# Edge softmax of a GNN layer: one product before the score matmuls in place of two behind them

## The reference, cut to what matters

```python
w_m = (efeat @ W_msg + b_msg).reshape(E, in_f, -1)
w_a = (efeat @ W_attn + b_attn).reshape(E, in_f, -1)
h_src = feat[src][:, :, None]
e1 = w_m * h_src
e2 = w_a * h_src
seg_max = jax.ops.segment_max(e2, dst, num_segments=N)
ex = jnp.exp(e2 - seg_max[dst])
denom = jax.ops.segment_sum(ex, dst, num_segments=N)
attn = ex / denom[dst]
ft = jax.ops.segment_sum(e1 * attn, dst, num_segments=N)
return ft.sum(axis=1)
```

## Time and profile before

| | us |
|---|---|
| three runs: median, lowest, highest | 5352.39, 5348.31, 5366.21 |
| the profiled execution's own time | 5326.47 |
| its span | 5324.7 |
| busy in it: PE, DVE, POOL, ACT | 3185.9, 3431.4, 3310.8, 1667.5 |
| first and last maximum scan (L1617) start | 51.7 and 1320.6 |

### The profile page before, as it was taken

How to read it: one execution, slowest core, us unless ns; L and a number is a source line. 1 busy time by engine, 2 the same in 40 slices (tenths; PEclk the granted TensorE clock), 3 DMA queues, 4 the chain that set the end, 5 groups by cost and what they waited for, 6 DMA issues and landing times. The chain is left out here.

```text
span 5324.7 us, 56203 instructions
## 1 busy us (share of the span) xinstructions
PE 3185.9 (60%) x12749; PEld 2452.6 (46%) x12749; DVE 3431.4 (64%) x5617; ACT 1667.5 (31%) x4309; POOL 3310.8 (62%) x2831
## 2 busy tenths in 40 slices
PE   6999999998344444199923223622223635566676
PEld 3444444444244444188822223522223425556675
DVE  7999999999765555588833334633334854444478
ACT  4666666666221111055510000210000331111135
POOL 4777777776478888799965654066553245555322
PEclk9999999999865555599955556855565655555588
DMA  3111111111333333523200000310000220000012
GB/s 105 44 44 44 44 44 46 45 44 29 111 73 59 59 59 57 91 63 85 73 15 5 6 5 4 95 14 5 5 5 3 76 72 5 6 5 6 4 55 78
DMA packets 399126, 224.63 MB, mean 42 GB/s; under 512 B 106218, under 2 KB 369198, under 8 KB 398978
## 3 DMA queue, kind: packets, MB, share of 16 engines
q1 hardware_dynamic: 279698, 203.40, 13.3%
q0 software_dynamic: 119296, 19.68, 6.2%
HBM read 158.12 MB, written 64.76 MB: 42 GB/s over the span
## 5 line engine op out<-in xcount | busy, mean ns | idle before, releaser
L1333 PE MATMUL ps<-arena 128*128 128x128 f32 x2976 | 659.0, 408 | 1061.8 <-DVE arena L1854 658.4
L1333 PEld LDWEIGHTS ps<-arena 128*128 128x128 f32 x2976 | 608.5, 310 | 1099.3 <-issue 1088.3
L758 POOL DMA_INDIRECT extra<-x_t,srci x784 | 760.4, 970 | 538.2 <-DVE arena L1871 277.5
L1237 PE MATMUL ps<-edge_in,wl 17*128 17x512 f32 x784 | 701.9, 1072 | 17.4 <-DVE arena L1623 8.7
L742 POOL DMA_INDIRECT sums<-cmb,sidx x392 | 613.9, 1566 | 139.1 <-issue 115.1
L758 POOL DMA_INDIRECT extra<-h_t,srci x392 | 370.7, 946 | 413.8 <-issue 293.6
L704 POOL DMA_INDIRECT xg<-in_x,xidx x392 | 478.5, 1221 | 221.0 <-issue 116.0
L691 POOL DMA_INDIRECT ft_t<-fts,fidx x392 | 507.7, 1295 | 143.4 <-issue 120.3
L1871 DVE TENSOR_TENSOR arena<-arena,ps 128x128 f32 x1488 | 426.9, 287 | 247.0 <-issue 69.6
L1017 ACT ACTIVATE ps<-extra 128x16 f32 x1392 | 165.1, 170 | 1314.4 <-issue 687.0
L1854 DVE TENSOR_TENSOR arena<-jmask,ps 128x1024 f32<-128x1024 f32 (+1 forms) x174 | 212.4, 1221 | 513.2 <-issue 316.1
(11 more groups left out here) (244 smaller groups left out, 6227.9 us busy)
## 6 DMA issues: line engine op xcount, KB each, us to landing
edge_in<-far_row SPq DMA_DIRECT2D x98, 256.0 KB
ain<-in_src_row SPq DMA_DIRECT2D x56, 448.0 KB
sums<-zero SPq DMA_DIRECT2D x132, 144.0 KB
arena<-rel_t SPq DMA_DIRECT2D x63, 256.0 KB
x_t<-yout SPq DMA_DIRECT2D x28, 448.0 KB, 3.4
xin<-x_t SPq DMA_DIRECT2D x28, 448.0 KB, 4.0
extra<-x_t,srci POOLq DMA_INDIRECT x784
ain<-x_t SPq DMA_DIRECT2D x28, 448.0 KB, 5.2
```

Source lines behind the costliest of these rows:

```text
L758: pool.indirect_dma_start(dy[:, t, :], None, table, bass.IndirectOffsetOnAxis(ap=srci[:, t:t + 1], axis=0)).then_inc(d_gathered[n % QUEUE] ...
L1237: last = pe.matmul(ps[k][:, h * ET:(h + 1) * ET], wl[:, (k * CH + h) * P:(k * CH + h + 1) * P], eft[b][:, :], start=True, stop=True)
L1333: last = pe.matmul(slot_sums(k, n)[:, j * P:(j + 1) * P], oneh[b][:, j * P:(j + 1) * P], placed[b][:, j * P:(j + 1) * P], start=True, stop ...
```

## The change

`h_src[i] * efeat[f]` is now formed once, before the matmuls: DVE multiplies the replicated features (`ps2`) by the edge features, which are loaded eight times over, on 128 rows (`make_outer`). PE contracts these 128 rows against `wl` for both scores, and adds the bias by two bf16 matmuls with the turned features, on 128 rows too (the bias in parts, `bias_first` and `bias_last`). DVE has no product behind either score. ACT no longer copies `ps2` to `hS`; its inverse goes into `ps2` instead, which the replication of a later tile overwrites only after the ratio has read it. The turned features are made twice (at rows 0 and 64 of zeroed buffers). The steps move: replication and attention scores are one tile ahead, turning two. ACT copies the carry columns ahead of the turned rows. The gather moves to even steps. Weights and turned features live in buffers of later stages.

```diff
 # SP
-            sp.dma_start(wl[:, :], wlog).then_inc(cst_in, 16)
-            sp.dma_start(repf, repcon).then_inc(cst_in, 16)
+            for j in range(PACK):
+                sp.dma_start(wl[j * F:(j + 1) * F, :], wlog[0:F, :]).then_inc(cst_in, 16)
+            sp.dma_start(bias_raw, wlog[F:F + 1, :].broadcast_to((P, 2 * CH * P))).then_inc(cst_in, 16)
+            wait(repf_zero, 1)
+            for r in part_bases:
+                sp.dma_start(repf[r:r + PARTS * F, :], repcon).then_inc(cst_in, 16)
...
-                    sp.dma_start(eft[b][:, :], ef[:, bass.ds((2 * i + c) * ET, ET)]).then_inc(main_in[b], 16)
+                    sp.dma_start(eft[b], ef[0:F, bass.ds((2 * i + c) * ET, ET)]
+                                 .unsqueeze(0).broadcast_to((PACK, F, ET))).then_inc(main_in[b], 16)
 # POOL
-                if c % 2:
-                    gather(i, c + 3)
+                if c % 2 == 0:
+                    gather(i, c + 4)
 # ACT, in step: removed
-                    act.wait_ge(h_ps, n + 1)
-                    if later(i, c, 1):
-                        act.wait_ge(e1_done, n)
-                    act.activation(flat(hS), ps[2][:, :], ACT.Copy).then_inc(h_sb, 1)
 # ACT, in step: behind the four activations of tile n
+                if inside(i, c - 2, TILES):
+                    act.wait_ge(ln_done, 2 * i + c - 2 + 1)
+                    if later(i, c - 2, 1):
+                        act.wait_ge(rat_done, 2 * i + c - 2)
+                    act.wait_ge(outer_done, 2 * i + c + 2 if inside(i, c + 1, TILES) else TILES)
+                    act.activation(inv, lnd[:, :, :], ACT.Exp, scale=-1.0).then_inc(inv_done, 1)
+                if c % 2:
+                    cast_x(i, c + 3)
 # PE, in step
+                replicate(i, c + 1)
+                transpose(i, c + 2)
+                scores(i, c + 1)
                 if inside(i, c, TILES):
...
+                    products(1, b).then_inc(e1_ps, 1)
+
+            def products(k, b):
+
+                for h in range(CH):
+                    o = ps[k][:, h * ET:(h + 1) * ET]
+                    cols = slice((k * CH + h) * P, (k * CH + h + 1) * P)
+                    pe.matmul(o, wl[:, cols], outer[b][:, h * ET:(h + 1) * ET], start=True, stop=False)
+                    pe.matmul(o, bias_first[:, cols], xT[b][:, :], start=False, stop=False)
+                    last = pe.matmul(o, bias_last[:, cols], xT[b][:, :], start=False, stop=True)
+                return last
 # DVE, in step
-                if c % 2:
-                    split(i, c + 1)
+                if c % 2 == 0:
+                    split(i, c + 2)
...
-                    dve.tensor_tensor(ps[0][:, :], ps[0][:, :], flat(hS), ALU.mult).then_inc(e2_done, 1)
...
-                    dve.wait_ge(wm_ps, n + 1)
-                    dve.tensor_tensor(flat(e1[b]), ps[1][:, :], flat(hS), ALU.mult).then_inc(e1_done, 1)
+                make_outer(i, c + 1)
...
-                    dve.scalar_tensor_tensor(body(qq), body(uu[o]), 1.0, e1[o], ALU.mult, ALU.mult).then_inc(q_done, 1)
+                    dve.wait_ge(e1_ps, m + 1)
+                    dve.scalar_tensor_tensor(body(qq), body(uu[o]), 1.0, e1p, ALU.mult, ALU.mult).then_inc(q_done, 1)
+            def make_outer(i, c):
...
+                dve.wait_ge(h_ps, n + 1)
+                dve.wait_ge(main_in[b], 32 * (nth(i, c) + 1))
+                if later(i, c, 2):
+                    dve.wait_ge(e1_ps, n - 1)
+                dve.tensor_tensor(outer[b].rearrange("p (h e) -> p h e", h=CH),
+                                  ps[2][:, :].rearrange("p (h e) -> p h e", h=CH),
+                                  eft[b].unsqueeze(1).broadcast_to((P, CH, ET)), ALU.mult).then_inc(outer_done, 1)
```

More of the change, by code:

```diff
@@ L892, in copy_xT @@
                 act.wait_ge(xT_ps, 2 * i + c + 1)
-                if later(i, c, 1):
-                    act.wait_ge(h_ps, 2 * i + c)
-                act.activation(xT[:, :], ps[3][0:PARTS * F, 0:ET], ACT.Copy).then_inc(xT_sb, 1)
+                if later(i, c, 2):
+                    act.wait_ge(e1_ps, 2 * i + c - 1)
+                for r in part_bases:
+                    last = act.activation(xT[c % 2][r:r + PARTS * F, :], ps[3][r:r + PARTS * F, 0:ET], ACT.Copy)
+                last.then_inc(xT_sb, 1)
             act.preload_act_table_set("natural_log_exp_and_others")
@@ L1227, in step @@
[L1227 to L1240, removed]
@@ new lines, in replicate @@
+            def replicate(i, c):
+                if not inside(i, c, TILES):
+                    return
+                n = 2 * i + c
+                pe.wait_ge(xT_sb, n + 1)
+                if later(i, c, 1):
+                    pe.wait_ge(outer_done, n)
+                if later(i, c, 4):
+                    pe.wait_ge(rat_done, n - 3)
+                for h in range(CH):
+                    last = pe.matmul(ps[2][:, h * ET:(h + 1) * ET], repsel[:, h * P:(h + 1) * P], xT[c % 2][:, :],
+                                     start=True, stop=True)
+                last.then_inc(h_ps, 1)
@@ L1243, in transpose, with scores @@
+            def scores(i, c):
+                if not inside(i, c, TILES):
+                    return
+                n = 2 * i + c
+                pe.wait_ge(outer_done, n + 1)
+                if later(i, c, 1):
+                    pe.wait_ge(w_done, n)
+                else:
+                    pe.wait_ge(w_made, TYPES)
+                    pe.wait_ge(bias_w, 10)
+                products(0, c % 2).then_inc(e2_ps, 1)
             def transpose(i, c):
@@ L1251, in transpose @@
                 for k in range(SUB):
-                    last = pe.matmul(ps[3][0:PARTS * F, k * P:(k + 1) * P],
-                                     high(xq[:, c % 2 * SUB + k, :, :].rearrange("p a f -> p (a f)")), identb[:, :],
-                                     start=True, stop=True)
+                    parts = high(xq[:, c % 2 * SUB + k, :, :].rearrange("p a f -> p (a f)"))
+                    for r in part_bases:
+                        last = pe.matmul(ps[3][r:r + PARTS * F, k * P:(k + 1) * P], parts, identb[:, :],
+                                         start=True, stop=True)
                 last.then_inc(xT_ps, 1)
             transpose(0, 0)
+            transpose(0, 1)
             turn_slots()
+            replicate(0, 0)
+            scores(0, 0)
             softmax_steps(pe, step)
@@ L1475, in _ @@
             dve.memset(eps_col[:, :], EPS).then_inc(zero_made, 1)
+            dve.memset(repf, 0.0).then_inc(repf_zero, 1)
+            for b in range(2):
+                dve.memset(ain[b][:, 0:ET // 2], 0.0).then_inc(repf_zero, 1)
             dve.memset(zero[:, :], 0.0).then_inc(zero_made, 1)
```

92 lines of the change are left out of this document (59 added, 33 removed).

## The result

| | before | after |
|---|---|---|
| median (lowest to highest), us | 5351.7 (4 runs beside the changed kernel) | 5291.2 (5249.7 to 5298.4, 4 runs) |
| ratio, 95% interval | | 0.987 (0.985 to 0.990) |
| profiled execution, its span | 5326.5, 5324.7 | 5295.6, 5293.8 |
| busy PE, DVE, POOL | 3185.9, 3431.4, 3310.8 | 2930.6, 3324.2, 3301.5 |
| first maximum scan starts | 51.7 | 53.7 |

The changed kernel is 60 us faster; 49 were forecast. The stage ends 59.5 us earlier. In the profiled executions the whole program gained only 31: the first weight load of L1420 (L1375 before) still starts 58.6 us earlier, at 2204.5, the last of L1378 (L1333 before) only 27.4, at 5070.6. The change touches nothing between them, the medians show the 60, and the four times of the changed kernel lie 49 apart, so that is taken as variation between executions; no run shows it apart.

What follows compares the result with a forecast made beforehand. The prediction took DVE to bound the softmax stage, at 26.25 us per two tiles. 5326.5 - 133 (product gone) + 72 (POOL binds) + 12 (start) = 5277.5, 5303 on the median; range 5222 to 5395.

Steps and rivals of the forecast that it cites:

- The `e2` product: Softmax stage, DVE: this product goes, 1.36 us in each of 98 tiles, -133 us.
- POOL becomes the bound: Softmax stage: POOL needs 25.2 to 25.3 us a pair of tiles against DVE's 23.53, giving back 72 us (11 to 114).
- x: Start of a POOL instruction behind the denominator scan's start, 0 to 1.27 us; a tile's loss is 3.02 - x.
- the steady phase: Softmax stage: x taken as 0.7 in a pair's first tile and 0.4 in its second, losses 2.3 and 2.6 us.
- PE hidden though its clock falls and rises in each tile: Softmax stage: the clock rises with matmuls on 128 rows, and even falling in every tile PE is just hidden.
- The start: Before the first tile: DMAs 3, DVE operations 5, later first scans 1.5 and 2.5; together +12 us, bounds 3 and 20.
- The sum: Whole program: 5326.5 - 133 + 72 + 12 = 5277.5 us, -49; on the median 5303.
- The rule of mutual blocking: DVE with two SBUF inputs and POOL block each other; scans held up too, 47 us, sum 5350; the prediction doubted it.
- The rule of busyness: PE's clock follows how busy it was, not rows; alone, nothing here would lift it, +301 us; the prediction doubted it.
- Rival 1: Softmax stage: POOL does not bind, so only -133 + 12 count, 5231 us; chance 0.20.

Runs made afterwards that it cites:

- e1: The changed kernel with two of the four scatters of a tile left out; ratio 0.9755 to the kernel before, -120 us.
- e3: The changed kernel with one more 128 x 512 product on DVE in each tile, which nothing reads; ratio 0.9888 to the kernel before, -56 us.
- e5: The changed kernel itself, unedited, measured again on another chip; ratio 0.9885 to the kernel before, -57 us.
- e12: The changed kernel with each of the two long scans of a tile issued as two halves; ratio 0.9768 to the kernel before, -113 us.
- e9: The kernel before with only its `e2` product on DVE left out; ratio 0.9831 to the kernel before, -81 us.
- e7: The kernel before with the score matmuls on operands of 128 rows in place of 17; ratio 0.9992 to the kernel before, -7 us.
- e8: The changed kernel with the bias and replication matmuls on 48 of the 128 rows; ratio 1.0919 to the kernel before, +479 us.
- e11: The changed kernel with the inverse back in SBUF; ratio 0.9878 to the kernel before, -59 us.

## Why the prediction was right, point by point

- **The `e2` product, -133.** Right: gone from the trace; `qq`, the outer product and the ratio keep 1.20 to 1.22.
- **POOL becomes the bound, +72.** Right in kind and size: pair 25.2 to 25.3 forecast, 25.16 in the mean, so 41 x 1.63 = 67. In the pair shown x is 0.76 and 0.42 where 0.7 and 0.4 were forecast, and the stalls 4.9 where 4.9. But the steady phase that the sum was worked out for isn't there: in the pair before x is 1.24 and 0.12 (603.83 and 614.49) and the stalls are 4.7, and in others an instruction starts just ahead of the scan and slips past it. That the mean came so close to one phase is in part luck; the bounds, 23.8 to 26.3, were what the argument carried. e1, e3 and e5 show the bound apart from DVE, e12 that the scans' length makes it. What failed in e9 is the generality, not this case.
- **PE hidden though its clock falls and rises in each tile.** Right, if barely, as it said: DVE waits for the replication in 13 tiles, 0.8 us as a rule, but such pairs are no longer than the others (571.50 to 596.02, 24.52). That rows were what held it down was argued from two stages; e7 and e8 showed it by edit.
- **The start, +12.** The mis-sized term: +2.0 to the first scan (51.67 to 53.72) and 2.3 on the second tile's wait (5.57 for 3.31), 4 in all between the two profiled executions. DVE's preparation did grow, its tables run from 16.66 to 22.3, but beside a wait: the operation behind them (L1608, L1540 before) starts at 32.16 after an idle 6.65, where it was 32.77 after 13.39. Now it follows PE's matmul of 31.75 (L1212); before, that matmul was done at 26.0, and what ended the wait is only `remote` in the trace. Nine DMAs and eight operations, 8 of the 12, were added up without asking what DVE did next; the longer chain of outer product and matmuls, the other 4, is what showed. In the other profiles the kernel before and its variants reach that scan at 45.0 to 51.9, the changed one and its variants at 52.7 to 54.5, so up to 9 can show, and the term isn't a constant.
- **The sum.** With what was measured: -133 + 67 + 4 = -62, where the stage ends 59.5 earlier.
- **The rule of mutual blocking** (the Trainium skill, "SBUF — State Buffer", "Who interferes with whom"). It gave 5350, and the trace doesn't agree: the time is 5291, and an instruction of POOL that is in flight when a scan begins (627.59, 0.46 us across the start of 628.10) delays no scan: 2.29 as ever. **The rule of busyness** (the Trainium skill, "TensorE: Matmul & The Clock Gate", "Part 1: The HAM clock gate"): e8, 93% busy and low, against the changed kernel, 79% busy and high for much of the tile, goes the other way than that rule alone would have it.
- Rival 1 (POOL does not bind, -121) is what e12 comes near to (-113), and with the scans in halves it is the better kernel: 1.1% (54 us) faster than e11 on the same chip, and 2.3% than the kernel before.

## What to carry to other kernels

When an engine close behind the bound shares it by stalls, price the change on that engine too: here half of the removed work came back because POOL had 5% of slack. Cut long operations that hold another engine into pieces where the waiting engine binds, and leave them whole where it doesn't: the same edit is worth some -54 us in one of these kernels and +12 in the other. A waiting engine's stalls are no constant: they depend on where its instructions fall in the other's step, so give them bounds and not one number. Before adding up work at the start, look what the engine waits for behind it.

## What the runs showed of the hardware

- An indirect DMA instruction of POOL that starts in a scan on two SBUF operands is served when the DVE instruction ends, even if the next is another such scan: 2.64 with a whole scan ahead, 1.69 with a half, at nearly the same offset. DVE's operation is not delayed (2.29). The turn lies close behind the scan's start: at 0.03 (630.78 in e12) and 0.01 (620.97 in e9) POOL takes its plain 0.97 and 0.95, and DVE's scans take 0.06 more (2.40 for 2.34, 2.35 for 2.29).
- Halving both scans costs DVE 0.10 to 0.17 us a tile: from the start of the first to that of the ratio 4.49 to 4.56, for 4.39.
- Rows of the bf16 operands, 48 in e8 and 128 after, decide the clock level with the order and columns of the matmuls the same: a pass of 128x512 f32 takes at least 1.06 throughout e8, and after two of them come down to 1.02. The column of the granted clock reads 1.00 in e8 and in the kernel before, whose durations are those of 1.2 GHz, and 0.78 after, where PE is faster. Here the durations of one shape tell the clock, not the column.
